# Gated MLP beside a scan: more feature tiles by block products, their operand sums in larger jobs

## The chip, the cores and the metric

The kernel runs on one core of a Trainium2 chip. Four engines compute: TensorE multiplies matrices, VectorE and ScalarE work element by element, GpSimd does the same on SBUF alone; SyncE issues the DMAs. SBUF is the on-chip memory (128 partitions), PSUM the accumulators that TensorE writes, HBM the memory behind the DMAs. The metric is device time in microseconds (us), the median of several runs.

## The reference

The input x is (8, 512, 512): eight batches of 512 rows, layer-normalised to xn. Two branches read xn, and the output is x plus their product.

```
xn = layernorm(x)
s  = ssm_branch(xn)              # input projection, conv, selective scan, output projection
g  = silu(ffn_branch(xn))
out = x + s * g

ffn_branch:  attn = causal attention(rmsnorm(xn) * ln1);  mod = 0.1 * tanh(attn @ A)
             h    = rmsnorm(xn) * ln2
             gate = silu(h @ W_in.T + mod * (h @ A) @ B)       # 2048 features
             up   = h @ W_up.T
             ffn  = xn + (gate * up) @ W_down.T
```

Products are fp32 made of three passes: each operand is a high part (fp32r, the form TensorE multiplies) and a low part, and high*high, high*low and low*high are summed in PSUM.

## The kernel before

The scan branch and the attention come first and are not touched. The gated MLP (gate, up, down) follows. Its 2048 features are 16 tiles of 128, and the eight batches have 512 rows each. A tile of one batch is called a step here.

Tiles 0 to 7 are computed directly, batch after batch (64 steps; four run inside the attention). In a step TensorE makes the gate and the up projection (`column`, helper `project3`, lines 72 to 74: 12 matmuls each, one more for the modulation at L2229), ScalarE the silu (L2279) and the high part GH (L2282), VectorE the product with up (L2302, which also frees the up bank) and the low part GL (L2304), and TensorE the 12 down matmuls (L2253 to L2255): 37 matmuls. After a batch's last step VectorE adds the sums in PSUM to the scaled skip rows (L2319) and SyncE stores them to `m_scratch`. SyncE loads the rows of each batch (FH, FL, 1 MB each) and the skip rows XT once a batch.

Tiles 8 to 15 are computed by a block scheme: two tiles and two batches form a 2x2 block matrix over halves of the 512 inputs, and seven products of blocks replace eight (the form with sums s1 to s4 of weight blocks and t1 to t4 of row blocks). One such group of 7 products for gate and for up, with modulation and 48 down matmuls, has 136 matmuls and stands for four steps of 37. There are 4 pairs of batches (`PAIRS`) times 4 pairs of tiles (`UNITS`): 16 block products. Each adds its down sums to MP in SBUF (`evict`, L2704), and after the last of a pair the rows are finished (silu, times s, plus x) and stored.

The operands of these products are sums of blocks, split in high and low. They are made during the direct steps, in `jobs`: 16 for rows (`rows`), 16 for weights (`weights`) and 4 for the down weights (`outward`), each in a buffer JOB of 8 KB a partition, two buffers in turn. SyncE loads a job (`load_job`, L2350 to L2359), GpSimd sums and splits it (`do_job`, L2385 to L2417), and SyncE stores the parts to scratch (`keep_job`, L2374, L2376), from where the block products load them as XB, SW and DW.

The order of everything is written out by hand in the generator `ffn_order`; every engine walks through the same list and does its part of each entry. SyncE therefore issues DMAs strictly in that order, and a DMA that waits for a semaphore holds all behind it. Before the first block product `second_ahead` waits until all jobs are stored, and loads XB0 to XB2 and SW0.

## Time and profile before

| | us |
|---|---|
| median of 3 runs | 2480.52 (2477.16 to 2482.77) |
| the profiled execution | 2479.31 |
| its span, first to last instruction | 2477.3 |
| TensorE busy | 2400.3 (97%) |
| VectorE, ScalarE, GpSimd busy | 1498.7, 1108.8, 708.8 |

In a row of the profile the columns are: start, duration, engine (PE is TensorE, DVE VectorE, ACT ScalarE, POOL GpSimd, SPq the queue of SyncE), line of the kernel, operation, tile written and tiles read, shape, count; in brackets the idle time before it and what ended that. Buffer numbers are left out of tile names (JOB stands for every JOB buffer). A busy PE means that matmuls follow each other without a gap: their recorded durations overlap, and the pitch from start to start is what a matmul costs.

### The profile page before, as it was taken

The page shows a single profiled execution, that of the slowest core. Times are in us where ns is not written, and L with a number is a line of the kernel's source. Part 1 is how long each engine was busy: PE and PEld are TensorE (multiplying, and loading weights), DVE is VectorE, ACT ScalarE, POOL GpSimd, SP SyncE. Part 2 cuts the span into 40 slices and gives each one's busy share as a digit, 9 for nine tenths or more (in the row PEclk, how much of TensorE's full clock was granted, in tenths as well). Part 3 has the DMA queues.
Part 4 walks back from the last instruction along what each step waited for, and adds up shares of the span by engine and source line. Part 5 has one row for each costly group of instructions (what it writes and reads, how often), then busy time and mean ns, then how long its engine had stood idle before and what let it go on. Part 6 is the DMA issues. An engine that isn't in the chain of part 4 may idle for free.

```text
span 2477.3 us, 37647 instructions
## 1 busy us (share of the span) xinstructions
PE 2400.3 (97%) x13847; PEld 1944.4 (78%) x13847; DVE 1498.7 (60%) x3000; ACT 1108.8 (45%) x1895; POOL 708.8 (29%) x674
## 2 busy tenths in 40 slices
PE   7999999999999899999999999999999999999998
PEld 5878878778888777777777678888888887787876
DVE  7857667667565588888988853223332345454546
ACT  6444544544444377777777641111111233332333
POOL 4000000000001244454453616664647002121212
PEclk9999999999999999999999899999999999999999
DMA  4000100000003577676666426655555945555461
GB/s 146 18 35 1 35 18 18 35 18 18 17 1 107 184 208 215 201 201 192 178 182 201 129 77 208 217 198 188 194 199 175 351 174 205 203 189 219 163 245 68
DMA packets 190747, 348.65 MB, mean 141 GB/s; under 512 B 19008, under 2 KB 89664, under 8 KB 181840
## 3 DMA queue, kind: packets, MB, share of 16 engines
q1 hardware_dynamic: 188064, 345.91, 42.6%
q8 instruction: 112, 1.84, 0.3%
q10 hardware_dynamic: 2496, 0.29, 0.1%
q14 instruction: 75, 0.61, 0.1%
HBM read 234.70 MB, written 111.15 MB: 140 GB/s over the span
## 4 chain that ended last, share of the span: by engine, by line
PE 80%; DVE 7%; issue 5%; DMA 4%; ACT 2%; POOL 2%; SPq 1%; DVEq 0%; ACTq 0%; POOLq 0%
PE PS L72 12%; PE PS L74 12%; PE PS L73 12%; PE PS L1748 3%; PE PS L813 2%; PE PS L812 2%; PE PS L814 2%; PE PS L2253 2%; PE PS L2254 2%; PE PS L2255 2%; PE PS L1706 2%; PE PS L1725 2%; PE PS L1707 2%; PE PS L1708 2%; PE PS L2612 2%
## 5 line engine op out<-in xcount | busy, mean ns | idle before, releaser
L1912 DVE CUSTOM_DVE_ANT_0 PS<-PS,MK 128x512 f32<-128x512 f32 (+3 forms) x512 | 244.4, 503 | 70.5 <-PE PS L1725 68.7
L1848 ACT ACTIVATE PF<-PS 128x512 f32<-128x512 f32 (+1 forms) x384 | 201.0, 528 | 90.5 <-PE PS L1752 60.0
L2302 DVE TENSOR_TENSOR SG<-SG,PS 128x512 f32<-128x512 f32 x60 | 41.3, 688 | 290.9 <-PE PS L74 289.7
L72 PE MATMUL PS<-XH,WH 128*128 128x512 f32 x504 | 208.8, 414 | 0.0
L74 PE MATMUL PS<-XH,WL 128*128 128x512 f32 x504 | 197.6, 392 | 0.0
L73 PE MATMUL PS<-XL,WH 128*128 128x512 f32 x504 | 196.8, 390 | 0.0
L74 PE MATMUL PS<-FH,GU 128*128 128x512 f32 x480 | 187.9, 391 | 0.0
L73 PE MATMUL PS<-FL,GU 128*128 128x512 f32 x480 | 187.5, 391 | 0.0
L72 PE MATMUL PS<-FH,GU 128*128 128x512 f32 x480 | 187.4, 390 | 0.0
L1725 PE MATMUL PS<-KS,QS 96*128 96x512 f32 (+3 forms) x512 | 172.4, 352 | 13.2 <-DVE MX L1912 13.1
L72 PE MATMUL PS<-XB,SW 128*128 128x512 f32 x448 | 175.5, 392 | 4.4 <-ACT P L2669 3.6
L1917 DVE TENSOR_TENSOR PL<-PF,PH 128x1024 f16<-128x1024 f32 (+1 forms) x128 | 175.4, 1370 | 4.1 <-ACT PH L1853 4.1
L74 PE MATMUL PS<-XB,SW 128*128 128x512 f32 x448 | 175.3, 391 | 0.0
L73 PE MATMUL PS<-XB,SW 128*128 128x512 f32 x448 | 175.0, 391 | 0.0
L1748 PE MATMUL PS<-QS,KS 97*128 97x512 f32 (+3 forms) x512 | 170.1, 374 | 0.0
L1089 DVE SCALAR_TENSOR_TENSOR XC<-PS,CW,XC 128x511 f32<-128x511 f32 (+2 forms) x192 | 143.6, 748 | 33.6 <-ACT XC L950 28.6
L1853 ACT CAST PH<-PF 128x1280 f16<-128x1280 f32 x128 | 161.2, 1260 | 4.1
L2012 POOL TENSOR_TENSOR PL<-PF,PH 128x256 f16<-128x256 f32 x112 | 91.8, 819 | 190.9 <-ACT PH L1853 190.6
L2279 ACT ACTIVATE SG<-PS 128x512 f32<-128x512 f32 x60 | 36.0, 601 | 243.4 <-PE PS L2229 243.3
L2764 POOL TENSOR_TENSOR U<-U,P 128x512 f32<-128x512 f32 x16 | 20.8, 1297 | 386.5 <-ACT P L2669 386.5
L657 POOL TENSOR_TENSOR RSTD<-VT,MHALF 128x4 f32<-128x4 f32 x8 | 8.1, 1012 | 417.9 <-DVE VT L576 417.9
L1725 PEld LDWEIGHTS PS<-KS,QS 96*128 96x128 f32 x512 | 100.6, 203 | 27.1 <-DVE MX L1912 22.1
(352 smaller groups left out, 6644.5 us busy)
## 6 DMA issues: line engine op xcount, KB each, us to landing
SW<-sw_scratch SPq DMA_DIRECT2D x10, 3584.0 KB, 12.3
qk_scratch<-QT SPq DMA_DIRECT2D x128, 256.0 KB, 4.7
QS<-qk_scratch SPq DMA_DIRECT2D x96, 256.0 KB, 4.0
KS<-qk_scratch SPq DMA_DIRECT2D x96, 256.0 KB, 4.0
xt_scratch<-JOB SPq DMA_DIRECT2D x32, 512.0 KB, 3.5
XB<-xt_scratch SPq DMA_DIRECT2D x16, 1024.0 KB, 6.3
sw_scratch<-JOB SPq DMA_DIRECT2D x32, 448.0 KB, 3.3
DW<-dw_scratch SPq DMA_DIRECT2D x10, 1024.0 KB, 5.0
```

The lines of the kernel that those rows point to most:

```text
L72: pe.matmul(o, lh(k), xh(k), start=open_ and k == 0, stop=False, skip_group_check=True)
L73: pe.matmul(o, lh(k), xl(k), start=False, stop=False, skip_group_check=True)
L74: last = pe.matmul(o, ll(k), xh(k), start=False, stop=close and k == nk - 1, skip_group_check=True)
L812: pe.matmul(PS[bank][:, :], YH[u][:, c], OH[:, d, :], start=d == 0, stop=False, skip_group_check=True)
L1089: dve.scalar_tensor_tensor(out=y[:, j:], in0=p[:, 0:S - j], scalar=CW[:, d, 3 - j:4 - j], in1=y[:, j:], op0=ALU.mult, op1=ALU.add).then_in ...
L1725: t = pe.matmul(PS[2 + a % 2][:, at:at + n], QS[0:96, h, 128 * how:n], KS[0:96, h, 0:n], start=how != 1, stop=True, skip_group_check=True)
L1748: t = pe.matmul(p[:, at:at + n], KS[0:97, h, 128 * J:128 * J + 128], QS[0:97, h, 128 * J:512], start=len(how) == 2 and at == 0, stop=len(h ...
L1848: act.activation(PE_[u][:, o:o + at], PS[4 + a % 2][:, 0:at], ACT.Exp, scale=SC).then_inc(a_ex, 1)
L1853: act.copy(PH[u][:, :], PE_[u][:, :]).then_inc(a_ph, 1)
L1912: dve.tensor_tensor_reduce(out=p, in0=p, in1=MK[:, 512 - n:512], scale=1.0, scalar=NEG, op0=ALU.add, op1=ALU.max, accum_out=MX[w % 2][:, j ...
L1917: dve.tensor_tensor(PL[u][:, 0:n], PE_[u][:, 0:n], PH[u][:, 0:n], ALU.subtract).then_inc(a_rm, 1)
L2012: pool.tensor_tensor(PL[u][:, 1024:1280], PE_[u][:, 1024:1280], PH[u][:, 1024:1280], ALU.subtract).then_inc(a_rp, 1)
```

## The change

Twelve tiles instead of eight are computed by block products: `FIRST` is 4 tiles directly and `UNITS` 6, so 24 block products instead of 16, and 32 direct steps (four inside the attention) instead of 64. The loads, scalings and splits of tiles 4 to 7 among the direct ones (`slice`) go. The jobs become 8 for rows, 12 for weights and 6 for down weights, in four buffers of 16 KB a partition: two for weights and down weights (class 0, `JOB0` and `JOB1`, summed by GpSimd) and two for rows (class 1, `JOB2` and `JOB3`, summed by VectorE in three parts, in three successive steps: L2377 to L2380, L2383 to L2387, L2390). A job's load is issued in the step after the store of the job that had its buffer, and still waits for that store to land. In the block product the extra modulation matmul goes to the bank DN[0] instead of ZG, and the first down matmul waits for the VectorE add that reads it.

```diff
-        GU.append(sb(re_, "GU1", [128, 4, 4, 512], F32R))
+        sb(re_, "GAP", [128, 8192])
+        js = ExitStack()
+        sb(js, "KEPT3", [128, 29576])
+        JOB = [sb(js, f"JOB{i}", [128, 4096], F32R) for i in range(2)]
+        sb(js, "KEPT4", [128, 4096])
+        JOB.append(sb(js, "JOB2", [128, 4096], F32R))
+        sb(js, "KEPT5", [128, 4096])
+        JOB.append(sb(js, "JOB3", [128, 4096], F32R))
+        js.close()
...
-        PAIRS, UNITS = NB // 2, 4
+        PAIRS, UNITS, FIRST = NB // 2, 6, 4
         ORDER = [u if p % 2 == 0 else UNITS - 1 - u for p in range(PAIRS) for u in range(UNITS)]
-        rows_jobs = [[("rows", p, k, t) for k in range(2) for t in range(2)] for p in range(PAIRS)]
-        unit_jobs = [[("weights", u, j, k) for j in range(2) for k in range(2)] + [("outward", u, 0, 0)] for u in range(UNITS)]
-        jobs = [job for u in range(UNITS) for job in rows_jobs[u] + unit_jobs[u]]
+        jobs = [[job for u in range(UNITS) for job in (("weights", u, 0), ("weights", u, 1), ("outward", u, 0))],
+                [("rows", p, k) for p in range(PAIRS) for k in range(2)]]
...
-            yield "slice", 6
+            yield "skips_scaled", 0
+            for w in range(2):
+                for n in range(2):
+                    yield "job_load", (w, n)
             yield "down", 3
-            ahead = 0
-            for q in range(EARLY + 1, 8 * NB):
-                b, f = divmod(q, 8)
+            later = {}
+            for q in range(EARLY + 1, FIRST * NB):
+                b, f = divmod(q, FIRST)
                 yield "column", q
                 yield "product", q
                 yield "down", q - 1
                 if f == 0 and b + 1 < NB:
                     yield "rows", b + 1
-                if f == 1 and b:
+                if f == 1:
                     yield "skips", b
-                if f == 6:
+                    if b == 1:
+                        yield "rows", 2
+                if f == 3:
                     yield "skips_scaled", b
-                if q == EARLY + 1:
-                    yield "slice", 7
-                if q >= 8 and q % 3 and ahead < len(jobs):
-                    if ahead == 0:
-                        yield "job", 0
-                    if ahead + 1 < len(jobs):
-                        yield "job", ahead + 1
-                    yield "job_kept", ahead
-                    ahead += 1
-            assert ahead == len(jobs)
+                i = q - EARLY - 1
+                for w, n in later.pop(i, ()):
+                    yield "job_load", (w, n)
+                if i % 4 == 0 and i // 4 < UNITS:
+                    for n in range(3 * (i // 4), 3 * (i // 4) + 3):
+                        yield "job", (0, n)
+                if i // 3 < len(jobs[1]):
+                    yield "job", (1, (i // 3, i % 3))
+                kept = []
+                if i >= 2 and i % 4 != 1 and (i - 2) // 4 < UNITS:
+                    kept.append((0, 3 * ((i - 2) // 4) + (i - 2) % 4))
+                if i and i % 3 == 0 and i // 3 <= len(jobs[1]):
+                    kept.append((1, i // 3 - 1))
+                for w, n in kept:
+                    yield "job_kept", (w, n)
+                    if n + 2 < len(jobs[w]):
+                        later.setdefault(i + 1, []).append((w, n + 2))
             yield "second_half", 0
-            yield "down", 8 * NB - 1
+            yield "down", FIRST * NB - 1
...
+        def load_job(sp, w, n):
+            kind, a, j = jobs[w][n]
+            r = 2 * w + n % 2
+            J = f32(JOB[r][:, :])
             if n >= 2:
-                sp.wait_ge(j_st[n % 2], j_st0[n % 2] + 32 * (n // 2))
-            else:
+                sp.wait_ge(j_st[r], j_st0[r] + 32 * (n // 2))
+            elif n == 0:
...
+                        c = 2048 * x + 1024 * b
+                        sp.dma_start(J[:, c:c + 1024].rearrange("p (k t) -> p k t", k=2),
+                                     f32(rows[2 * a + b])[:, j::2, :]).then_inc(j_ld[r], 16)
...
+                    sp.dma_start(J[:, 512 * f:512 * f + 512], (WgT, WuT)[j][FIRST + 2 * a + f]).then_inc(j_ld[r], 16)
...
+                    sp.dma_start(J[:, 512 * f:512 * f + 512], wd_[FIRST + 2 * a + f]).then_inc(j_ld[r], 16)
...
+                high, low = (J[:, c:c + 2048].rearrange("p (i t) -> p i t", i=4) for c in (0, 2048))
+                to = [f32(xt_d[a])[:, :, x, j, :] for x in range(2)]
...
+                high, low = (J[:, c:c + 1792] for c in (2048, 0))
+                to = [f32(sw_d[a])[:, j, x, :, :, :].rearrange("p i k m -> p (i k m)") for x in range(2)]
...
+                high, low = (J[:, c:c + 1024].rearrange("p (f m) -> p f m", f=2) for c in (2048, 0))
                 to = [f32(dw_d[a])[:, :, x, :] for x in range(2)]
...
+            sp.wait_ge(j_op[w], j_op0[w] + job_ops(w, n) - 1)
+            sp.dma_start(to[0], high).then_inc(j_st[r], 16)
+            sp.wait_ge(j_op[w], j_op0[w] + job_ops(w, n))
+            sp.dma_start(to[1], low).then_inc(j_st[r], 16)
...
+        def sum_rows(dve, n, part):
+            r, op, op0 = 2 + n % 2, j_op[1], j_op0[1] + 7 * n
+            R_, J = JOB[r][:, :], f32(JOB[r][:, :])
+            b11, b21, b12, b22, t1, t2, t3, t4 = (J[:, 512 * i:512 * i + 512] for i in range(8))
+            if part == 0:
+                dve.wait_ge(j_ld[r], j_ld0[r] + job_loads(1, n))
+                dve.tensor_tensor(J[:, 0:2048], J[:, 0:2048], J[:, 2048:4096], ALU.add).then_inc(op, 1)
+                dve.wait_ge(op, op0 + 1)
+                dve.tensor_tensor(t1, b12, b11, ALU.subtract).then_inc(op, 1)
+                dve.tensor_tensor(t3, b22, b12, ALU.subtract).then_inc(op, 1)
+            elif part == 1:
+                dve.wait_ge(op, op0 + 2)
+                dve.tensor_tensor(t2, b22, t1, ALU.subtract).then_inc(op, 1)
+                dve.wait_ge(op, op0 + 4)
+                dve.tensor_tensor(t4, b21, t2, ALU.subtract).then_inc(op, 1)
+                dve.wait_ge(op, op0 + 5)
+                dve.tensor_copy(R_[:, 0:2048], J[:, 2048:4096]).then_inc(op, 1)
             else:
...
+                dve.wait_ge(op, op0 + 6)
+                dve.tensor_tensor(R_[:, 2048:4096], J[:, 2048:4096], J[:, 0:2048], ALU.subtract).then_inc(op, 1)
...
+        def sum_weights(pool, n):
+            kind, a, j = jobs[0][n]
+            r, op, op0 = n % 2, j_op[0], j_op0[0] + (job_ops(0, n - 1) if n else 0)
+            R_, J = JOB[r][:, :], f32(JOB[r][:, :])
+            pool.wait_ge(j_ld[r], j_ld0[r] + job_loads(0, n))
+            if kind == "weights":
+                w0, w1 = (J[:, c:c + 512].rearrange("p (k m) -> p k m", k=4) for c in (0, 512))
+                a11, a12, a21, a22, s1, s2, s4 = (J[:, 256 * i:256 * i + 256] for i in range(7))
+                pool.tensor_tensor(w0, w0, l2b(), ALU.mult).then_inc(op, 1)
+                pool.tensor_tensor(w1, w1, l2b(), ALU.mult).then_inc(op, 1)
+                pool.wait_ge(op, op0 + 2)
+                pool.tensor_tensor(s1, a21, a22, ALU.add).then_inc(op, 1)
+                pool.wait_ge(op, op0 + 3)
+                pool.tensor_tensor(s2, s1, a11, ALU.subtract).then_inc(op, 1)
+                pool.wait_ge(op, op0 + 4)
+                pool.tensor_tensor(s4, a12, s2, ALU.subtract).then_inc(op, 1)
+                pool.tensor_tensor(a21, a11, a21, ALU.subtract).then_inc(op, 1)
+                pool.wait_ge(op, op0 + 6)
+                pool.tensor_copy(R_[:, 2048:3840], J[:, 0:1792]).then_inc(op, 1)
+                pool.wait_ge(op, op0 + 7)
+                pool.tensor_tensor(R_[:, 0:1792], J[:, 0:1792], J[:, 2048:3840], ALU.subtract).then_inc(op, 1)
+            else:
+                pool.tensor_copy(R_[:, 2048:3072], J[:, 0:1024]).then_inc(op, 1)
+                pool.wait_ge(op, op0 + 1)
+                pool.tensor_tensor(R_[:, 0:1024], J[:, 0:1024], J[:, 2048:3072], ALU.subtract).then_inc(op, 1)
...
+            for r in range(4):
+                sp.wait_ge(j_st[r], j_st0[r] + 32 * len(range(r % 2, len(jobs[r // 2]), 2)))
+            sp.wait_ge(m_u, FIRST * NB - FIRST)
...
-                pe.wait_ge(n_ad, n_ad0 + 5 * v + 1)
-                modulate(pe, ZG, f1, b1, True).then_inc(n_pr, 1)
+                pe.wait_ge(*((n_ev, 8 * v - 3) if v else (m_fn, 4 * NB - 1)))
+                modulate(pe, DN[0], f1, b1, True).then_inc(n_pr, 1)
...
-                    if t < 2:
-                        pe.wait_ge(*((n_ev, 8 * v - 3 + t) if v else (m_fn, 4 * NB - 1 + t)))
+                    if t == 0:
+                        pe.wait_ge(n_ad, n_ad0 + 5 * v + 3)
...
```

On SyncE, in the second batch of direct steps in which jobs run, the order before is this. `a_q` and `a_k` are semaphores of landed stores, `a_lg` counts GpSimd's operations, `m_fn` VectorE's additions at the end of a batch.

```order
L2350 DMA JOB0<-rh_scratch 128x2x256 [waits a_q]
L2350 DMA JOB0<-rh_scratch 128x2x256
L2350 DMA JOB0<-rl_scratch 128x2x256 x2
L2374 DMA xt_scratch<-JOB1 512x1x256 [waits a_lg]
L2376 DMA xt_scratch<-JOB1 512x1x256 [waits a_lg]
L2350 DMA JOB1<-rh_scratch 128x2x256 [waits a_k]
```

The same place now, from the store of the first rows job on; `a_nu` counts VectorE's operations on row jobs, and `a_wt` is a semaphore of landed stores too.

```order
L2367 DMA xt_scratch<-JOB2 512x1x512 [waits a_nu]
L2369 DMA xt_scratch<-JOB2 512x1x512 [waits a_nu]
L2201 DMA XT0<-in_x_dram 128x512 [waits m_fn]
L2201 DMA XT1<-in_x_dram 128x512 [waits m_fn]
L2201 DMA XT2<-in_x_dram 128x512 [waits m_fn]
L2201 DMA XT3<-in_x_dram 128x512 [waits m_fn]
L2348 DMA JOB1<-in_WgT_dram 128x512 [waits a_k]
L2348 DMA JOB1<-in_WgT_dram 128x512
L2344 DMA JOB2<-rh_scratch 128x2x512 [waits a_wt]
L2344 DMA JOB2<-rh_scratch 128x2x512
L2344 DMA JOB2<-rl_scratch 128x2x512 x2
L2367 DMA dw_scratch<-JOB0 256x1x512 [waits a_lg]
```

Both classes of jobs now share the one queue, transfers are twice as long a row, and a load of rows stands behind loads and stores of weights.

On VectorE, around the end of a batch, the direct steps before:

```order
L2302 TENSOR_TENSOR SG0<-SG0,PS2 128x512 [waits m_u,m_sg]
L2304 TENSOR_TENSOR GL0<-SG0,GH0 128x512 [waits m_gh]
L2319 TENSOR_TENSOR M10<-XT0,PS4 128x512 [waits m_m0,m_xn,a_th,m_dn]
L2319 TENSOR_TENSOR M11<-XT1,PS5 128x512 [waits m_xn,m_m1]
L2319 TENSOR_TENSOR M12<-XT2,PS6 128x512 [waits m_xn,m_m2]
L2319 TENSOR_TENSOR M13<-XT3,PS7 128x512 [waits m_xn,m_m3]
L2302 TENSOR_TENSOR SG1<-SG1,PS3 128x512 [waits m_u,m_sg]
```

And now, from the last of these additions on; `a_ni` and `a_ti` are semaphores of landed loads of row jobs.

```order
L2311 TENSOR_TENSOR M13<-XT3,PS7 128x512 [waits m_xn,m_m3]
L2377 TENSOR_TENSOR JOB3<-JOB3 128x2048 [waits a_ni]
L2379 TENSOR_TENSOR JOB3<-JOB3 128x512 [waits a_nu]
L2380 TENSOR_TENSOR JOB3<-JOB3 128x512
L2292 TENSOR_TENSOR SG1<-SG1,PS3 128x512 [waits m_u,m_sg]
L2294 TENSOR_TENSOR GL1<-SG1,GH1 128x512 [waits m_gh]
L2383 TENSOR_TENSOR JOB3<-JOB3 128x512 [waits a_nu]
L2385 TENSOR_TENSOR JOB3<-JOB3 128x512 [waits a_nu]
L2387 CAST JOB3<-JOB3 128x2048 [waits a_nu]
```

Seven operations of a row job, the first of which waits for a DMA, now stand in VectorE's queue between the products of the steps.

## Rows read from the trace of the kernel before

**Rows 1.** Busy time by stage: stretch, length, busy us of each engine, PEclk, DMA share, GB/s

```profile
1458.00:1958.00 500.00, 500.00 (x2193) 412.03 (x2193) 159.73 (x190) 76.42 (x126) 261.60 (x248) 1.00 0.58 195
1958.00:2477.00 519.00, 499.64 (x2179) 408.44 (x2178) 263.34 (x373) 170.39 (x288) 90.39 (x63) 0.99 0.52 193
```

**Rows 2.** Waits in 1458 to 2477: engine, line, releaser: total us, times, longest

```profile
DVE SG L2302 <- PE PS L74: 289.7, 57, 6.4
...
PE PS L2612 <- DVE HH L2743: 4.5, 3, 1.5
PE PS L72 <- ACT P L2669: 3.6, 3, 1.2
```

**Rows 3.** TensorE in order of time: first direct step that remains, first block product

```profile
1457.84 0.39 PE L72 MATMUL PS<-FH,GU 128*128 128x512 f32 x1
...
1958.52 0.39 PE L72 MATMUL PS<-XB,SW 128*128 128x512 f32 x1
...
2009.66 0.39 PE L2612 MATMUL PS<-DW,HH 128*128 128x512 f32 x1
```

**Rows 4.** VectorE in order of time: end of modulation, two steps, two block products

```profile
1456.55 0.68 DVE L1958 TENSOR_TENSOR MS<-PS,MS 16x512 fp32r<-16x512 f32 x1 [3.05 <-ACT MS L1882]
...
1522.91 0.69 DVE L2302 TENSOR_TENSOR SG<-SG,PS 128x512 f32<-128x512 f32 x1 [6.37 <-PE PS L74]
...
1531.35 0.69 DVE L2302 TENSOR_TENSOR SG<-SG,PS 128x512 f32<-128x512 f32 x1 [5.40 <-PE PS L74]
...
2000.96 0.69 DVE L2712 TENSOR_TENSOR G<-G,PS 128x512 f32<-128x512 f32 x1 [10.54 <-PE PS L74]
...
2007.69 0.67 DVE L2728 TENSOR_TENSOR U<-U,PS 128x512 f32<-128x512 f32 x1
...
2031.97 0.69 DVE L2712 TENSOR_TENSOR G<-G,PS 128x512 f32<-128x512 f32 x1 [10.54 <-PE PS L74]
```

**Rows 5.** DMA in 4 us from 2224.4, then from 1632.4, then from 2140.4

```profile
DMA packets 835, 1.53 MB, mean 382 GB/s; under 512 B 90, under 2 KB 90, under 8 KB 835
q1 hardware_dynamic: 835, 1.53, 103.0%
...
DMA packets 215, 1.63 MB, mean 408 GB/s; under 512 B 16, under 2 KB 16, under 8 KB 16
...
DMA packets 64, 1.84 MB, mean 459 GB/s; under 512 B 0, under 2 KB 0, under 8 KB 0
```

**Rows 6.** SyncE's queue: the second store of a job, the load behind it

```profile
1525.42 0.55 SPq L2376 DMA_DIRECT2D xt_scratch<-JOB  x1
1528.85 1.22 SPq L2350 DMA_DIRECT2D JOB<-rh_scratch  x2
```

**Rows 7.** GpSimd in order of time, operations of the jobs

```profile
1648.25 0.73 POOL L2390 TENSOR_TENSOR JOB<-JOB 128x256 f32<-128x256 f32 x1
...
1653.78 0.62 POOL L2401 TENSOR_TENSOR JOB<-JOB,L2C 128x256 f32<-128x256 f32 x1
...
1657.07 0.93 POOL L2411 CAST JOB<-JOB 128x896 fp32r<-128x896 f32 x1
1658.09 2.12 POOL L2413 TENSOR_TENSOR JOB<-JOB 128x896 fp32r<-128x896 f32 x1
```

**Rows 8.** GpSimd and VectorE in order of time, one operation of each

```profile
1709.67 2.40 POOL L2417 TENSOR_TENSOR JOB<-JOB 128x1024 fp32r<-128x1024 f32 x1
...
1709.96 2.66 DVE L2304 TENSOR_TENSOR GL<-SG,GH 128x512 fp32r<-128x512 f32 x1 [0.69 <-ACT GH L2282]
```

**Rows 9.** DMA issues on the page: engine, count, KB each, us to landing

```profile
SW<-sw_scratch SPq DMA_DIRECT2D x10, 3584.0 KB, 12.3
...
DW<-dw_scratch SPq DMA_DIRECT2D x10, 1024.0 KB, 5.0
```

**Rows 10.** Three stretches of TensorE: length, busy us, PEclk, DMA share, GB/s

```profile
1390.00:1394.00 4.00, 3.50 (x41) 1.00 0.69 238
1394.00:1398.00 4.00, 0.66 (x4) 0.74 0.01 2
1398.00:1402.00 4.00, 4.00 (x22) 0.50 0.42 136
```

More of the change, by code:

```diff
@@ L2192, in ffn_sync @@
                         sp.dma_start(XT[u][:, :], xn_[4 * n + u]).then_inc(m_t[u], 16)
-                elif kind == "job":
-                    load_job(sp, n)
+                elif kind == "job_load":
+                    load_job(sp, *n)
                 elif kind == "job_kept":
-                    keep_job(sp, n)
+                    keep_job(sp, *n)
                 elif kind == "second_half":
                     second_ahead(sp)
-                elif kind == "down" and n % 8 == 7:
-                    h = n // 8
+                elif kind == "down" and n % FIRST == FIRST - 1:
+                    h = n // FIRST
                     for u in range(4):
@@ L2310, in ffn_vector @@
                                           ALU.subtract, ALU.mult).then_inc(m_xn, 1)
-                elif kind == "down" and q % 8 == 7:
-                    h = q // 8
+                elif kind == "job" and q[0] == 1:
+                    sum_rows(dve, *q[1])
+                elif kind == "down" and q % FIRST == FIRST - 1:
+                    h = q // FIRST
                     dve.wait_ge(m_dn, q + 1)
@@ L2325, in ffn_pool, with job_loads, job_ops @@
                     attn_pool(pool, [("inverse", n, None)])
-                elif kind == "job":
-                    do_job(pool, n)
+                elif kind == "job" and n[0] == 0:
+                    sum_weights(pool, n[1])
             second_pool(pool)
-        def job_loads(n):
-            return sum(64 if jobs[i][0] == "rows" else 32 for i in range(n % 2, n + 1, 2))
-        def job_ops(n):
-            return sum({"rows": 7, "weights": 8, "outward": 2}[jobs[i][0]] for i in range(n + 1))
-        def load_job(sp, n):
-            kind, a, j, k = jobs[n]
-            J = f32(JOB[n % 2][:, :])
+        def job_loads(w, n):
+            return (32, 64)[w] * (n // 2 + 1)
+        def job_ops(w, n):
+            return sum({"rows": 7, "weights": 8, "outward": 2}[jobs[w][i][0]] for i in range(n + 1))
+        def load_job(sp, w, n):
+            kind, a, j = jobs[w][n]
+            r = 2 * w + n % 2
+            J = f32(JOB[r][:, :])
             if n >= 2:
-                sp.wait_ge(j_st[n % 2], j_st0[n % 2] + 32 * (n // 2))
-            else:
+                sp.wait_ge(j_st[r], j_st0[r] + 32 * (n // 2))
+            elif n == 0:
                 sp.wait_ge(a_mo, 2 * NB)
@@ L2361, in keep_job @@
[L2361 to L2363 removed]
+                    sp.dma_start(J[:, 512 * f:512 * f + 512], wd_[FIRST + 2 * a + f]).then_inc(j_ld[r], 16)
+        def keep_job(sp, w, n):
+            kind, a, j = jobs[w][n]
+            r = 2 * w + n % 2
+            J = f32(JOB[r][:, :])
             if kind == "rows":
[L2365 to L2366 removed]
+                high, low = (J[:, c:c + 2048].rearrange("p (i t) -> p i t", i=4) for c in (0, 2048))
+                to = [f32(xt_d[a])[:, :, x, j, :] for x in range(2)]
@@ L2431, in load_unit @@
         def load_unit(sp, u, free):
-            if free is None:
-                sp.wait_ge(m_u, 60 if u == 0 else 8 * NB)
-            else:
+            if free is None and u:
+                sp.wait_ge(m_u, FIRST * NB)
+            elif free is not None:
                 sp.wait_ge(n_pr, 15 * (free + 1))
@@ L2437, in load_unit @@
                          f32(sw_d[u]).rearrange("p a b c d e -> p (a b c d e)")).then_inc(n_sw[u % 2], 16)
-            if free is None:
-                sp.wait_ge(m_dn, 58 + 2 * u)
-            else:
+            if free is not None:
                 sp.wait_ge(n_dd, 8 * (free + 1))
@@ L2480, in second_ahead @@
         def second_ahead(sp):
-            for r in range(2):
-                sp.wait_ge(j_st[r], j_st0[r] + 32 * len(range(r, len(jobs), 2)))
-            sp.wait_ge(m_u, 56)
+            for r in range(4):
+                sp.wait_ge(j_st[r], j_st0[r] + 32 * len(range(r % 2, len(jobs[r // 2]), 2)))
+            sp.wait_ge(m_u, FIRST * NB - FIRST)
             for i in range(3):
@@ L2760, in second_pool @@
                 if v and v % UNITS == 0:
-                    for n in range(2 * v - 8, 2 * v):
+                    for n in range(8 * (v // UNITS) - 8, 8 * (v // UNITS)):
                         skipped(n)
```

173 lines of the change are left out of this document (46 added, 127 removed).

## The prediction

> **What bounds the kernel now.** I read the busy time by stage first. From 1458 to 1958 us (direct steps) TensorE is busy all 500.00 us at the full granted clock, from 1958 to 2477 (block products) 499.64 of 519; VectorE has 160 and 263 us of work there, GpSimd 262 and 90, and the DMA engines are busy 0.58 and 0.52 of the time [rows 1]. The list of waits says the same from the other side: VectorE waits 289.7 us for TensorE, while TensorE's two waits for others are 4.5 and 3.6 us in all, at the three ends of a pair [rows 2]. So the matmuls' pitch is the bound, and DMAs and sums hide behind it. The reader should keep the two middle figures in mind: 195 GB/s now [rows 1], and no packet size of this kernel that goes far beyond 400 GB/s [rows 5].
>
> The profiled execution took 2479.31 us, its span of 2477.3 and 2.0 around it; the median is 1.2 above it, which is inside the scatter of the runs. I count from the span.
>
> **TensorE.** VectorE's product of one step and that of the next are 1531.35 - 1522.91 = 8.44 us apart, those of two block products 2031.97 - 2000.96 = 31.01 [rows 4]. Each of the 8 new block products takes the place of four steps: 31.01 - 4 x 8.44 = -2.75 us, by eight -22.0. (136 matmuls for 148, 12 x 0.228 = 2.74, agrees.) The first remaining direct step starts at 1457.84 [rows 3]; 27 of the 32 steps follow from there. 27 steps of 8.44 and some 2.7 for the last step's down matmuls (12 x 0.228) bring the first block product to 1688.4 if nothing holds TensorE, and the end of the span to 2455.3.
>
> **Slices and DN[0].** The scalings and splits of tiles 4 to 7 that go ran on engines that wait for TensorE: 0. The wait for DN[0] costs nothing by the old place: the VectorE add that it waits for ends at 2008.36 [rows 4], 1.3 us before the first down matmul at 2009.66 [rows 3]; plus or minus 1 us at the four pair ends. With six products to a pair, one SW and one DW load, 12.3 and 5.0 us [rows 9], lie in 31.0 us: hidden, 0.
>
> **DMA in the direct stage.** Here the change does most. The direct stage shrinks from 500 us to 231, but its bytes don't. The first job loads stand behind the end of the modulation (1456.55 + 0.68 [rows 4]), so everything below falls between 1457.2 and the first block product, which needs SW0, and SW0 stands behind the last store of the jobs:
> - in packets of 2 KB: eight row jobs, 2.10 MB in and 2.10 out, 33.6 MB; weight loads 12 x 0.52 = 6.3; down weights 6 x 1.57 = 9.4; seven batches of skip rows, 7.3; seven stores of M1, 7.3. Together 64.0 MB;
> - in larger packets: weight stores 12 x 1.835 = 22.0 MB, rows of batches 2 to 7 12.6, XB0 to XB2 3.1, SW0 3.7. Together 41.4.
>
> 105.3 MB in 231 us would be 456 GB/s, with no idle moment. With the queue full this trace shows 382 GB/s for 2 KB packets, 408 for the larger ones of the steps, and 459 only for the 28 KB packets of SW [rows 5]. So: 64.0/0.385 = 166 us (I take 385, as the short view's 382 has its edges in it), 22.0/0.408 = 54, 12.6/0.408 = 31, 3.1/0.400 = 8, 3.7/0.455 = 8: 267 us.
>
> To it come stretches in which the queue is empty. SyncE waits for a store to land before it may issue the load that takes the buffer, and holds all behind it: after the second store of a job was issued the next load came 3.43 us later [rows 6], of which the transfer is 1.4, so 2.0 us idle. Of 22 such gates I find seven where the store awaited was the last thing issued (behind weight jobs 2, 5, 11 and 14, row jobs 2 and 3, and before the first XB): 14 us. At the start SyncE stands at the M1 stores of a batch until TensorE has finished it: 6 us. Landing of SW0: 1.5. 267 + 14 + 6 + 1.5 = 288.5, so the first block product starts at 1745.7 instead of 1688.4: +57.
>
> TensorE can't run ahead of this: sums of row jobs stand in VectorE's queue between the products that free the PSUM banks, so a row load that is late by more than some 8 us stops the steps; and what is not held there is held before the first block product. Bounds: everything at 459 GB/s and no gate gives 1457.2 + 229.4 + 7.5 = 1694, +6; everything at 2 KB rates with the wait of 2.0 at all 22 gates 1457.2 + 276 + 44 + 7.5 = 1785, +96.
>
> A rule of the notes bears on this rate. The Trainium skill, "DMA: Bandwidth & Descriptors", section Bandwidth, has large transfers measured at 341 GB/s for 1 MB and 425 for 16 MB. By 425 the 105.3 MB take 248 us and the kernel ends near 2485, by 341 they take 309 and it ends near 2546, each without the terms that follow; the trace's 382 to 408 lies between them.
>
> **GpSimd late with a sum.** A weight job is two scalings of 512 (1.24 each), four sums of 256 (0.73), a cast of 1792 (1.86) and a subtraction of 1792 (4.24), twice the widths of [rows 7] where they doubled: 10.3, with gaps 11.4 us. Down weights 3.5; a unit 26.3. When an operation of VectorE on SBUF overlaps, one of the two stands still: GL took 2.66 us beside a GpSimd subtraction [rows 8], and 0.69 is usual. Now VectorE sums rows there too: 16 widths of 512 at 0.67 [rows 4] are up to 10.7 us a job. With these between, I take 16.5 us for a weight job. SyncE then comes to its store before it is summed in four places of every twelve steps, by some 3, 4.5, 4.5 and 8 us: 20 us for a repetition. Twelve steps are half of the job schedule, which would make 40; part of it is taken up by gates and start already counted. I take +20, bounds 0 and +40.
>
> **Restart.** The first block products come after TensorE has stood still, and DMAs of the first pair (XB3 behind DW0 and the eight MP loads) are late by some 2.5 us. After a stretch with 0.66 us of work in 4 the granted clock was 0.74 and then 0.50, that is 1.2 of 2.4 GHz [rows 10]. I take +4, bounds 0 and +8.
>
> **Sum.** 2477.3 - 22.0 + 57 + 20 + 4 = 2536.3; with 2.0 outside 2538 us. The far ends of all terms are 2463 and 2601. The forecast's own range is 2500 to 2575.
>
> **Rivals.**
> - *The DMAs keep pace.* TensorE stays gapless and only the -22.0 counts: 2457 us, up to 2475 if the first pair starts late. For it: DMA is at 0.58 now, and no store in the old stage holds TensorE. Against: it needs 456 GB/s through the whole stage, and 61% of the bytes are in packets that were never seen above 385. Chance 0.07.
> - *DMA bound, but gates and sums hide.* If all packets go at 408 or a little better and deeper backlog covers the gates, the stage takes 105.3/0.408 + 7.5 = 265.6 us, the first block product starts at 1722.8, +34: 2491, and 2476 at the better end, where gain and loss are about even. For it: four buffers and loads issued a step late leave more in the queue than before. Against: six of the seven gates follow directly from the order. Chance 0.11, 0.04 of it for no change.
> - *The engines' exclusion is the bound.* GpSimd's 26.3 us, 4/3 row jobs of VectorE (14.3) and its four GL (2.8) are 43.4 us for four steps of 33.8, if they never overlap; with some 8 us more in which sums wait for transfers and not the other way round, 51. Six units: 6 x (51 - 33.8) = 103, in place of 57 + 20: 2455.3 + 2.0 + 103 + 6 + 4 = 2570, to 2600 with the gates. For it: [rows 8]. Against: that row is one pair of operations, and most of VectorE's operations there read PSUM. Chance 0.14. The Trainium skill, "SBUF — State Buffer", calls the shared ports an exclusive lock whose loser fully blocks; [rows 8] agrees for this one pair.
>
> **How the numbers follow.** The forecast has 0.68. A measurement here tells 0.2% (5 us) from no change. Faster: 0.07, the first rival; same: 0.04, the better end of the second; slower: all else, 0.89. The range from 2480 to 2592 leaves out the first rival, the second's best end, and the far end of the third.
>
> **What would show it.** Right: the stage from 1458 to the first block product lasts some 288 us, with DMA busy 0.9 or more at about 370 to 385 GB/s; TensorE has gaps in it that end with VectorE's product, which stood behind a row sum that waited for its load; SyncE's longest waits are for landed stores and for GpSimd's sums; block products keep 31.0 us. The lock is the bound instead if DMA share stays near 0.75 while GpSimd's subtractions last 6 us and more and VectorE's casts several us. Wrong altogether: a direct stage of about 231 us with TensorE gapless, or block products that last longer than 31 us.

## The result, and the profile after

The changed kernel takes 2538.52 us (2537.01 to 2540.75), the kernel before on the same chip 2479.15 (four runs; 2480.52 above was the median of three): a ratio of 1.0239, 95% interval 1.0221 to 1.0256. The prediction was 2538. The profiled execution has a span of 2536.1 us.

The busy time by stage of the kernel after [rows 1 has it for before]: the direct steps until the first block product, the last part of that stretch by itself, and the block products.

```profile
1738.00:1767.50 29.50, 0.00 (x0) 0.00 (x0) 4.57 (x8) 0.00 (x0) 0.00 (x0) 0.54 0.95 374
1457.00:1767.50 310.50, 238.60 (x999) 192.37 (x998) 190.85 (x174) 32.08 (x54) 173.32 (x108) 0.90 0.91 340
1767.50:2536.10 768.60, 748.87 (x3264) 613.82 (x3264) 378.05 (x537) 246.57 (x416) 113.22 (x79) 0.99 0.49 185
```

TensorE, gapless in that stage before, has 71.9 us of gaps there now, 29.5 of them at the end, where it does nothing at all. The DMA engines are busy 0.91 of the stage, at 340 GB/s where it was 195. The block products are as they were: 768.6 us for 24 against 518.8 for 16 [rows 3 and the span], 31.2 for each of the eight new ones. VectorE's rows there answer to [rows 4], at the same pitch of 31.01; the add of U3 (L2727) ends at 2009.31, 1.3 us before the first down matmul (L2611 now) at 2010.63, as before.

```profile
2001.92 0.69 DVE L2711 TENSOR_TENSOR G<-G,PS 128x512 f32<-128x512 f32 x1 [10.54 <-PE PS L74]
2008.64 0.67 DVE L2727 TENSOR_TENSOR U<-U,PS 128x512 f32<-128x512 f32 x1
2032.93 0.69 DVE L2711 TENSOR_TENSOR G<-G,PS 128x512 f32<-128x512 f32 x1 [10.54 <-PE PS L74]
```

```profile
2010.63 0.39 PE L2611 MATMUL PS<-DW,HH 128*128 128x512 f32 x1
```

The waits of the kernel after from 1455 to 1800 us, in total, times and longest [rows 2 has before's]. L2259 is the first down matmul of a step, L2294 VectorE's GL, L2311 the additions of M1, L2377 the first sum of a row job.

```profile
DVE JOB L2377 <- DMA JOB<-rl_scratch: 48.0, 7, 12.5
...
PE PS L72 <- DMA SW<-sw_scratch: 31.3, 1, 31.3
PE PS L2259 <- DVE GL L2294: 23.8, 5, 14.6
...
PE PS L2259 <- DVE M L2311: 15.4, 3, 7.6
```

VectorE stands at row sums for their loads, TensorE for VectorE, and at the end TensorE for SW0. SyncE's own waits in that stretch: L2212 are the M1 stores, L2344 to L2351 loads that wait for a store to land, L2369 a store that waits for a sum.

```profile
SPq L2348 <- DMA sw_scratch<-JOB: 30.4, 4, 10.1
SPq L2212 <- DVE M L2311: 30.3, 12, 20.8
SPq L2348 <- DMA dw_scratch<-JOB: 28.3, 5, 8.8
SPq L2344 <- DMA xt_scratch<-JOB: 18.9, 4, 8.5
SPq L2369 <- POOL JOB L2412: 17.0, 6, 5.7
```

The DMA queue of the kernel after from 1457 to 1767.5: packets, MB, share of the 16 engines.

```profile
q1 hardware_dynamic: 39295, 105.31, 91.0%
```

105.31 MB, as predicted, in 0.910 x 310.5 = 282.6 us of transfer, 373 GB/s where I had counted 267 us. (The Trainium skill, "DMA: Bandwidth & Descriptors", section Bandwidth, has 341 and 425 GB/s measured for loads of 1 and 16 MB; the 373 lies between.)

### The profile page after: what moved, and what is told of

It is laid out like the page before. It is cut to its first block, busy times and chain, and to the rows that moved or that the text cites. A ratio compares the mean times of both kernels' runs of the same rounds, so it can differ in the third digit from the quotient of the medians.

```text
span 2536.1 us, 37627 instructions
## 1 busy us (share of the span) xinstructions
PE 2387.7 (94%) x13751; PEld 1929.0 (76%) x13751; DVE 1639.1 (65%) x3140; ACT 1137.7 (45%) x1947; POOL 643.6 (25%) x550
## 4 chain that ended last, share of the span: by engine, by line
PE 69%; DMA 9%; DVE 8%; issue 5%; POOL 3%; SPq 3%; ACT 2%; DVEq 0%; ACTq 0%; POOLq 0%
PE PS L72 10%; PE PS L74 10%; PE PS L73 10%; PE PS L2611 3%; PE PS L2612 3%; PE PS L2613 3%; PE PS L1748 2%; PE PS L813 2%; PE PS L812 2%; PE PS L814 2%; PE PS L1706 2%; DMA xt_scratch<-JOB 2%; PE PS L1725 2%; PE PS L1707 2%; PE PS L1708 2%
## 5 line engine op out<-in xcount | busy, mean ns | idle before, releaser
L72 PE MATMUL PS<-XB,SW 128*128 128x512 f32 x672 | 264.0, 393 | 34.9 <-DMA SW<-sw_scratch 31.3
L74 PE MATMUL PS<-XB,SW 128*128 128x512 f32 x672 | 263.4, 392 | 0.0
L73 PE MATMUL PS<-XB,SW 128*128 128x512 f32 x672 | 263.1, 392 | 0.0
L2763 POOL TENSOR_TENSOR U<-U,P 128x512 f32<-128x512 f32 x24 | 31.9, 1329 | 607.2 <-ACT P L2668 607.2
L2711 DVE TENSOR_TENSOR G<-G,PS 128x512 f32<-128x512 f32 x24 | 16.5, 687 | 249.5 <-PE PS L74 249.5
L72 PEld LDWEIGHTS PS<-XB,SW 128*128 128x128 f32 x672 | 126.7, 189 | 65.5 <-DMA SW<-sw_scratch 31.7
L2703 DVE TENSOR_TENSOR MP<-MP,PS 128x512 f32<-128x512 f32 x192 | 129.2, 684 | 72.2 <-PE PS L2613 72.1
L2611 PE MATMUL PS<-DW,HH 128*128 128x512 f32 x384 | 149.6, 390 | 5.3 <-DVE U L2727 5.3
L2613 PE MATMUL PS<-DW,HH 128*128 128x512 f32 x384 | 149.4, 389 | 0.0
L2612 PE MATMUL PS<-DW,HH 128*128 128x512 f32 x384 | 149.4, 389 | 0.0
L73 PEld LDWEIGHTS PS<-XB,SW 128*128 128x128 f32 x672 | 126.8, 189 | 27.5
L74 PEld LDWEIGHTS PS<-XB,SW 128*128 128x128 f32 x672 | 126.9, 189 | 27.2
## 6 DMA issues: line engine op xcount, KB each, us to landing
sw_scratch<-JOB SPq DMA_DIRECT2D x24, 896.0 KB, 10.3
```

What stands on the lines that cost most here:

```text
L72: pe.matmul(o, lh(k), xh(k), start=open_ and k == 0, stop=False, skip_group_check=True)
L73: pe.matmul(o, lh(k), xl(k), start=False, stop=False, skip_group_check=True)
L74: last = pe.matmul(o, ll(k), xh(k), start=False, stop=close and k == nk - 1, skip_group_check=True)
L2611: pe.matmul(bank[:, :], high, DW2[u % 2][:, f, 0, :], start=f == 0, stop=False, skip_group_check=True)
L2612: pe.matmul(bank[:, :], high, DW2[u % 2][:, f, 1, :], start=False, stop=False, skip_group_check=True)
L2613: last = pe.matmul(bank[:, :], low, DW2[u % 2][:, f, 0, :], start=False, stop=f == 1, skip_group_check=True)
```

## The experiments

Theory D: the stage is bound by its 105 MB of transfers. Theory L: by GpSimd and VectorE shutting each other out. Theory Q: by SyncE's order, in which loads wait for landings, stores for sums, and M1 stores for TensorE. Theory R, formed after the first four runs, is one loop of Q. D+Q, formed after e8, has transfers and order side by side, each covering what the other gives back. The runs come from four sessions, each beside the kernel before on the same chip (medians 2476.1 to 2479.4), so they are compared by their ratios. "First block product" is its place in the profiled execution; MB and share are those of the DMA queue from 1457 us to there, as in the row above.

| | ratio to before | first block product | MB, share |
|---|---|---|---|
| the changed kernel | 1.0239 (1.0221 to 1.0256) | 1767.5 | 105.3, 0.91 |
| e1 sums 32 wide | 1.0249 (1.0231 to 1.0267) | 1757.2 | 104.6, 0.93 |
| e2 fewer bytes | 1.0137 (1.0112 to 1.0162) | 1734.1 | 76.4, 0.76 |
| e3 rows from SBUF | 1.0255 (1.0236 to 1.0275) | 1762.2 | 88.1, 0.78 |
| e4 8 KB stores | 1.0252 (1.0235 to 1.0269) | 1765.6 | 105.3, 0.90 |
| e5 third buffer | 1.0262 (1.0239 to 1.0284) | 1768.8 | 105.8, 0.91 |
| e7 = e3 + e5 | 1.0202 (1.0178 to 1.0226) | 1753.6 | 88.9, 0.81 |
| e8 = e7 + late M1 stores | 1.0109 (1.0085 to 1.0132) | 1730.1 | 88.1, 0.85 |
| e9 late M1 stores only | 1.0216 (1.0193 to 1.0240) | 1762.1 | 105.9, 0.91 |
| e10 = e8 + first loads early | 1.0126 (1.0103 to 1.0148) | 1721.1 | 82.7, 0.84 |
| e13 = e8 + fewer bytes | 1.0075 (1.0057 to 1.0092) | 1733.6 | 65.9, 0.65 |
| e11 six tiles direct | 0.9993 (0.9982 to 1.0004) | | |
| e12 = e11, sums spread | 1.0001 (0.9992 to 1.0010) | 1829.9 | |

**e1_sums_32_wide.** All sums of jobs narrow, here the longest two of VectorE:

```diff
-                dve.tensor_tensor(J[:, 0:2048], J[:, 0:2048], J[:, 2048:4096], ALU.add).then_inc(op, 1)
+                dve.tensor_tensor(J[:, 0:32], J[:, 0:32], J[:, 2048:2080], ALU.add).then_inc(op, 1)
...
-                dve.tensor_copy(R_[:, 0:2048], J[:, 2048:4096]).then_inc(op, 1)
+                dve.tensor_copy(R_[:, 0:32], J[:, 2048:2080]).then_inc(op, 1)
```

> All sums of jobs keep their number and order but are 32 columns wide (GpSimd's first two jobs whole), so they take almost no time; every load and store is as in the changed kernel. The scratch operands are not the reference's. Theory D (the direct stage is bound by its 105 MB of DMA; the engines' exclusion costs only the stretches in which SyncE waits for a sum): of the 34 us in which the DMA engines lack work some 8 to 20 go, 2518 to 2530 us. Theory L (GpSimd and VectorE shut each other out, and that sets the stage): the whole loss of some 77 us goes, 2478 or less.

Measured 2534.96, ratio 1.0249: no change. GpSimd's work in the stage fell from 173 to 44 us, VectorE's from 191 to 87, and the time stayed, above D's 2518 to 2530 too. While 105 MB go, the sums are not the bound: L falls for the changed kernel, and with it my term of +20 for late sums as an addition. What the sums cost once the bytes are fewer e1 can't say. The stage by engine and the DMA queue of e1 from 1457 to 1757.2:

```profile
1457.00:1757.20 300.20, 238.40 (x988) 191.93 (x986) 87.09 (x171) 31.74 (x53) 43.81 (x106) 0.91 0.93 349
```

```profile
q1 hardware_dynamic: 38929, 104.59, 93.1%
```

0.931 x 300.2 = 279.5 us of transfer: with the sums gone the transfers fill what was left. (The profiled execution was the shortest of e1's four, 2527.24, so the first block product at 1757.2 flatters it.)

**e2_a_third_fewer_bytes.**

```diff
-                high, low = (J[:, c:c + 1792] for c in (2048, 0))
+                m = 448 if a else 1792
+                high, low = (J[:, c:c + m] for c in (2048, 0))
```

> All sums whole, all DMAs in their number, order and waits, but from the second unit and pair on the stores carry a quarter (down weights whole), row loads half of their bytes: about 75 MB instead of 105 until the first block product. The block products read the first unit's and the first pair's operands, in size as before. Theory D: 75 MB at 360 to 380 GB/s are 197 to 208 us, under the 231 that TensorE needs, so most of the loss goes: 2459 to 2480 us. Theory L: sums are as wide as before, 2525 or more. Theory Q (SyncE's order: a load waits for a store to land, a store for a sum, whatever the bytes): each of 22 gates keeps its 2 us and the waits for sums stay, some 2500 to 2515.

2508.54, ratio 1.0137: some 25 us of 60 come back, less than D had said and inside what Q had. Against the changed kernel it is the only run that takes away nothing but bytes, 29 MB of 105.

**e3_rows_from_sbuf.**

```diff
-                dve.tensor_tensor(J[:, 0:2048], J[:, 0:2048], J[:, 2048:4096], ALU.add).then_inc(op, 1)
+                for x in range(2):
+                    dve.wait_ge(m_r[x], 32 * (a + 1) - (0 if x else 16))
+                    dve.tensor_tensor(J[:, 1024 * x:1024 * x + 1024].rearrange("p (k t) -> p k t", k=2),
+                                      f32(FH[x])[:, j::2, :], f32(FL[x])[:, j::2, :], ALU.add).then_inc(op, 1)
```

> Row jobs add FH and FL of both batches of a pair where they lie in SBUF, instead of loading the same rows again: 16.8 MB of loads and eight gates less, sums as wide as before, outputs the reference's. Theory D: 16.8 MB at 359 GB/s are 47 us, and 88.5 MB take some 234, about what TensorE needs; with 10 to 20 us of gates and start 2466 to 2490 us. Theory L: the same VectorE and GpSimd work on SBUF, 2530 or more. Theory Q: the eight gates of the row loads and what stands behind them, 15 to 25 us, so 2513 to 2523.

2535.99, ratio 1.0255: nothing, although 17 MB less went. D alone falls too; Q's 2513 to 2523 is missed as well, and only L's "2530 or more" holds, which e1 speaks against. But the edit does more than take loads away: the two row jobs of a pair are now summed within five steps of every eight, and since the sums read FH and FL, SyncE may load a later batch's rows only after them, which is a new wait. SyncE's waits in e3 until 1762.2 (L2221 M1 stores, L2357 weight loads, L2377 and L2379 job stores, L2204 the rows of batch 2, which here wait for VectorE's sum):

```profile
SPq L2221 <- DVE M L2320: 36.2, 12, 20.2
SPq L2357 <- DMA sw_scratch<-JOB: 31.7, 5, 10.8
SPq L2379 <- POOL JOB L2432: 30.9, 8, 4.6
SPq L2377 <- POOL JOB L2430: 30.4, 7, 6.1
SPq L2357 <- DMA dw_scratch<-JOB: 29.7, 5, 9.3
SPq L2204 <- DVE JOB L2396: 12.5, 1, 12.5
```

They add up to 171 us of a stage of 305, while the DMA engines are busy only 0.78 of it. The loads that went are missing where SyncE stands longest: from 1460 to 1500 the DMA share is 0.44 in e3 and 0.82 in the changed kernel, with the new wait of 12.5 us and one of 20.2 at the M1 stores in that stretch. How much of the 17 MB's gain the new wait took was not tried. And the weight jobs run in a loop. e3 in order of time, the last store of a unit's second weight job, the load that waits for it to land, and GpSimd's first sum on that load:

```profile
1593.33 0.56 SPq L2379 DMA_DIRECT2D sw_scratch<-JOB  x1
...
1606.61 0.80 SPq L2357 DMA_DIRECT2D JOB<-in_WgT_dram  x2
...
1610.55 1.23 POOL L2420 TENSOR_TENSOR JOB<-JOB,L2C 128x512 f32<-128x512 f32 x1 [3.92 <-DMA JOB<-in_WgT_dram]
```

Three jobs a unit in two buffers: the next unit's first weight job gets the buffer of the one summed last, 17 us from store to sum. The DMA queue was busy 0.965 of the 22 us from 1590 on, so most of these 17 us are transfers of other loads and stores.

**e4_xt_8_kb_stores.**

```diff
-        xt_d = nc.dram_tensor("xt_scratch", [4, 128, 4, 2, 2, S], F32R, kind="Internal").ap()
+        xt_d = nc.dram_tensor("xt_scratch", [4, 128, 2, 2, 4, S], F32R, kind="Internal").ap()
```

> The scratch of the row jobs is laid out so that a store writes 8 KB a partition in one piece instead of four of 2 KB; the loads of XB1 to XB6 read 2 KB pieces instead. Bytes, sums and waits stay. Theory D with packets as the price: 16.8 MB of stores at 400 to 408 instead of 359 GB/s are 4 to 6 us less in the direct stage, XB1 and XB2 give back 0.7: 2533 to 2535 us, and the block products stay at 31.0. Theories L and Q: 2538, within 1.5.

2537.27, ratio 1.0252. A gain of 4 us would not stand out from this scatter, so the time is inconclusive on the price of packets. The queue's own row shows it: 33923 packets instead of 39295, and 0.901 x 308.5 = 278.0 us of transfer instead of 282.6, about what was expected. It is the time that did not follow.

**e5_third_buffer.** (third buffer in the place of STGC; load and store counts follow)

```diff
-            r = 2 * w + n % 2
+            r = 2 + n % 2 if w else (0, 1, 4)[n % 3]
```

> The changed kernel with a third buffer for class 0 (12 KB a partition in the place of STGC, which is dead by then): a unit's two weight jobs and its down weights each have a buffer, so the load of the next unit's first weight job no longer waits for the store of the second one. Bytes, sums and operations stay. Theory R (ring: the two buffers and three jobs a unit make a loop of load, two sums, landing of the store, load, of some 42 us in e3 and 46 to 48 in the changed kernel, against 33.8 of four steps; the transfers of 105 MB, some 281 us, are a second bound of about the same size): the ring goes, the transfers stay, first block product 1745 to 1757, 2513 to 2527 us. Theory D alone (bytes): 2530 to 2540, as e3 should have fallen by then and didn't, so it is weak. Theory Q (SyncE's waits for sums and landings in general): 2530 or more.

2543.00, ratio 1.0262: a miss for R, nothing gained; Q had 2530 or more. With all bytes on the way the loop isn't what is late.

**e7_rows_from_sbuf_third_buffer.** Both edits.

> e3 (rows from SBUF, 16.8 MB less) and e5 (third buffer) together, outputs the reference's. Theory R with the second bound: both are relieved, 88.5 MB in some 236 us, with 15 to 30 us of start and gates the first block product at 1708 to 1723: 2477 to 2492 us, that is 45 to 60 less than either part alone leaves. Theory Q: SyncE's standing at M1 stores and at sums stays, 2505 to 2525.

2527.60, ratio 1.0202. Neither edit alone gained; together they give some 9 us (1.0239 to 1.0202 of 2479, with intervals that just overlap), far from the 45 to 60 expected of R, and 3 us above Q's range too. The loop is a small part of Q.

**e8_both_late_m1_stores.**

```diff
+                if f == 0:
+                    yield "skips_kept", b - 1
...
-                elif kind == "down" and n % FIRST == FIRST - 1:
-                    h = n // FIRST
+                elif kind == "skips_kept":
+                    h = n
```

> e7 with the M1 stores of a batch at the end of SyncE's part of that step instead of in front of its loads and job stores (SyncE stood there for 20 us in the first batch and 30 to 36 in all). Theory R: the first down weights load and the first stores go out some 15 us earlier, 5 to 12 us less than e7, 2468 to 2485. Theory Q: 20 us and more less than e7.

2504.59, ratio 1.0109: 23 us less than e7, by nothing but the place of a batch's four small stores in one queue, as Q had said. SyncE's wait at them fell from 69.4 us in e7 to 11.3; a part of it moved to the wait that e3's edit brought in, for VectorE's row sums ahead of a batch's rows, 12.4 us in e7:

```profile
SPq L2212 <- DVE JOB L2404: 28.2, 3, 12.8
SPq L2229 <- DVE M L2328: 11.3, 11, 4.9
```

**e9_only_late_m1_stores.** The same edit on the changed kernel.

> The changed kernel with only the M1 stores moved to the end of SyncE's part of a step (the edit that gave 23 us from e7 to e8). Theory D+Q (two paths of about the same length side by side: the transfers, 281 us when all 105 MB go, and SyncE's order with its standing at M1 stores, sums and landings; each alone covers what the other gives back): only the start goes, where the DMA engines idled 6.5 us, so 2528 to 2537 us. Theory Q alone (SyncE's order sets the stage): 20 us and more, 2518 or less.

2531.22, ratio 1.0216: 5.7 us by the ratios, with intervals that overlap. The edit worth 23 us in e8 is worth a quarter of that by the medians while 105 MB go: here transfers cover the order. This is inside the 2528 to 2537 that D+Q had said beforehand, and above Q's 2518.

**e10_first_loads_early.**

```diff
+                if i == 25:
+                    yield "first_loads", 0
```

> e8, and SW0 and XB0 to XB2 are loaded as soon as the weight jobs that shared their place are stored, ahead of the last row stores, DW0 and MP; the load of batch 2's rows stands behind the first job's store (SyncE waited there 12.8 us for VectorE). Theory D+Q: TensorE's wait of 22 us before the first block product in e8 shrinks to some 5, and the start gains a few us: 2482 to 2492 us. If transfers are still the bound at the end of the stage, the wait only moves into the first pair (XB3, DW0, MP): 2495 to 2505.

2508.32, ratio 1.0126, not better than e8, and above both ranges expected. TensorE of e10, from 1700 to 1800:

```profile
1721.06 0.76 PE L72 MATMUL PS<-XB,SW 128*128 128x512 f32 x1 [6.07 <-issue]
1749.08 0.79 PE L72 MATMUL PS<-XB,SW 128*128 128x512 f32 x1 [16.87 <-DMA XB<-xt_scratch]
```

The first block product comes 9 us earlier than in e8, and TensorE waits 16.87 us for the next XB instead: the wait moved into the first pair, the way of the second case, 3 us past its range.

**e13_e8_third_fewer_bytes.** e2's cut of the stores on e8.

> e8 (twelve tiles, row sums from SBUF, third buffer, late M1 stores) with the cut of e2's stores: from the second unit and pair on a quarter of their bytes, some 65 MB instead of 88. The block products read the first unit's and pair's operands. Theory D+Q (transfers and SyncE's order together were the whole loss): TensorE's 231 us are the bound, first block product at 1690 to 1702, 2459 to 2471 us, which shows TensorE's term of -22. If the sums or their exclusion hold TensorE, 2480 or more.

2499.69, ratio 1.0075: a miss for D+Q; "2480 or more" was the case in which sums hold TensorE. (The profiled execution was the longest of e13's four, and e8's the shortest of its four.) The queue and TensorE's waits until 1733.5:

```profile
q1 hardware_dynamic: 26317, 65.91, 65.2%
```

```profile
PE PS L2276 <- DVE M L2328: 13.3, 3, 6.4
PE PS L2276 <- DVE GL L2311: 9.8, 1, 9.8
```

22 MB less than e8 bring some 8 us, with intervals that overlap and the DMA engines idle a third of the time. What holds TensorE there is VectorE, 23.1 us of waits, whose products stand behind row sums, and SW0. SyncE's longest wait in e13 is for the row sums too, the one that e3's edit brought in:

```profile
SPq L2212 <- DVE JOB L2406: 47.8, 3, 19.8
```

In the longest of the three, from 1597.5 to 1617.4, the DMA engines are busy 0.09 of the time, VectorE 19.1 us of 19.9 and GpSimd 17.2, and VectorE's four scalings of XT take 8.15 us where one takes 0.56 on average in e1. So theory L, which e1 excludes for the changed kernel, stands again as a rival for what is left here. Of the changed kernel's 59 us some 40 are shown to belong to bytes and SyncE's order; which edit would bring the rest is open. e1's narrow sums were not tried on e13, and no run cut bytes to 66 MB without the new wait.

**e11_six_tiles_direct.** Ten tiles by block products.

```diff
-        PAIRS, UNITS, FIRST = NB // 2, 6, 4
+        PAIRS, UNITS, FIRST = NB // 2, 5, 6
```

> Ten tiles by block products instead of twelve: six direct tiles (48 steps), five units, 20 block products, row sums from SBUF as in e3, M1 stores late as in e8, one buffer for weight jobs, one for down weights, one for rows; outputs the reference's. By TensorE's term alone 4 x -2.75 = -11.0 against the kernel before: 2466 of span, 2468 us, if the stage of 43 steps (363 us for some 85 MB, 235 GB/s) hides all transfers and sums; TensorE then has no gap over 2 us. Theory D+Q: nothing is late with that much room, 2466 to 2474. If VectorE's row sums hold TensorE at the ends of batches even so, 2475 to 2485.

2475.41 against 2476.77 of the kernel before, ratio 0.9993: the same, where 11 us less were expected.

**e12_six_tiles_sums_spread.**

```diff
-                for x in range(3):
-                    row_parts[12 * p - 3 + 4 * n + x] = [(2 * p + n, x)]
+                row_parts[12 * p - 2 + 4 * n] = [(2 * p + n, 0)]
+                row_parts[12 * p - 1 + 4 * n] = [(2 * p + n, 1), (2 * p + n, 2)]
```

> e11 (six direct tiles, ten by block products) with the row sums of the first pair a step apart from each other's stores (the second row job starts at step 3, its parts follow at 6 and 7, batch 2's rows are loaded at step 3) and those of the later pairs in steps in which GpSimd has no weight job, down weights a step earlier, row stores first in SyncE's part of a step. In e11 three stalls of TensorE (2.05, 2.72, 2.17 us) and the halved clock behind them took 11 us between 1500 and 1600 us, as much as the four block products give. Without them 2464 to 2470 us; if VectorE and GpSimd still meet, 2471 to 2476.

2479.42, ratio 1.0001: a miss. TensorE of e12, and the stretch of 100 us around its first wait, then the same stretch of the kernel before:

```profile
1566.54 0.79 PE L2293 MATMUL PS<-DW,GH 128*128 128x512 f32 x1 [3.24 <-DVE GL L2342]
...
1772.68 0.50 PE L2293 MATMUL PS<-DW,GH 128*128 128x512 f32 x1 [1.39 <-DVE GL L2342]
...
1841.59 0.50 PE L72 MATMUL PS<-XB,SW 128*128 128x512 f32 x1 [3.20 <-DMA XB<-xt_scratch]
```

```profile
1500.00:1600.00 100.00, 96.76 (x419) 79.26 (x418) 60.24 (x57) 13.93 (x23) 43.52 (x27) 0.98 0.55 200
```

```profile
1500.00:1600.00 100.00, 100.00 (x440) 82.38 (x440) 27.58 (x31) 14.44 (x24) 68.41 (x64) 1.00 0.67 219
```

440 matmuls before, 419 in e12. One wait of 3.24 us cost 21 x 0.228 = 4.8 us: its next matmul is recorded with 0.79 us instead of 0.39. The same count, matmuls missing against the pitch of 0.228, gives 0.5 us from 1600 to 1700, 1.6 to 1800, 0.7 to 1829.9 and 5.2 to 1860, where the wait for XB is: with the first some 13 us, against the 12 by which the span of 2478.5 misses the 2466 that TensorE's term gives. The pair ends cost what they did before (9.2 us of waits, 8.9 before). So in this execution the waits and the clock behind them account for about all of the loss. Neither version beats the kernel before.

## Why the prediction was right, point by point

The forecast of 2538 met the time. Its main mechanism held, that the bytes of the jobs no longer fit into the shorter stage (e2); that late sums and gates add to the transfers did not (e1, e8, e9), and that the total came out all the same is luck.

**TensorE, -22.0.** Held: 31.2 us for each new block product where 31.01 was counted, and the same pitch. But no run shows the -22 alone, since no kernel with twelve tiles has a median under 2499.

**DN[0] and the slices, 0.** Held. The waits at the pair ends are 5.3 and 2.5 us where before they were 4.5 and 3.6 [rows 2]:

```profile
PE PS L2611 <- DVE U L2727: 5.3, 3, 1.8
PE PS L72 <- ACT P L2668: 2.5, 3, 1.0
```

**Transfers, +57.** The bytes were right (105.31 for 105.3 MB), the speed was not: 373 GB/s over the stage instead of 394 (105.3 in 267 us), so 282.6 us. The share of 0.91 came as named, the 370 to 385 GB/s only for the time in which the queue was busy; over the whole stage it was 340. A part of the error is a reading: the 382 GB/s stand beside a queue at 103.0% [rows 5], that is 371 for a full queue, and 385 was taken. (The 2485 and 2546 given beside this sum hold 7.5 us of start and landing and the +4, and leave out the 14 us of gates.)

**GpSimd late, +20.** This step failed. The lateness came: SyncE waited 25 us in all for GpSimd's sums (17.0, 6.4 and three short ones). But e1 takes it away and the time stays, so what I added to the transfers lies beside them. In the stage the queue was without work for 310.5 - 282.6 = 27.9 us, where 41.5 were counted (21.5 for gates and start, 20 here), and the transfers took 15.6 more than counted. The first block product at 1767.5 against my 1765.7 is luck: two errors of opposite sign, some 16 and some 14 us. The sum behind the 20 is wrong too: the operations of a weight job listed there add up to 11.5 us, not 10.3, and the 16.5 taken with overlaps were 13.1 on average, from first to last operation, in the trace of the kernel after.

**Gates and start, +21.5, as an addition.** Also mis-stated. I took SyncE's standing for holes in a stream of transfers. e8 and e9 show that it is a chain beside them: the same edit of the order gives 23 us where 17 MB are gone and a third buffer is in, and 6, with intervals that overlap, where all bytes go. So I read the stage as following the longer of two chains, 283 us of transfers with their few holes, and SyncE's order. For the order no run gives a length: e3's stage of 305 us at a share of 0.78 holds a wait of 12.5 us that e3 itself brings in, and in e2, with every wait of the changed kernel, the stage lasts 277. SyncE's longest wait was not for a landing or a sum, as I had said, but for the M1 stores, 20.8 us. The chains are not independent (a landing is a transfer, so fewer bytes in the stores shorten the order too), and their exact shares stay open. Of the three runs with twelve tiles whose time was expected by this reading, e9 came out as said, e10 and e13 did not; in e13 the sums may be a third chain, which no run tested. The 6 us of the start and the 1.5 of SW0's landing have no row behind them, and no run tried them alone. The +57 was no price per byte: in e2 the transfers are 72 us shorter (0.761 x 277.1 = 210.9), and 25 us come back.

**Restart, +4.** 768.6 against 766.9 us counted from the first block product: +1.7.

**The rivals.** The DMAs did not keep pace. The one by which gates hide (2491) is excluded by the time. The exclusion of VectorE and GpSimd is real for single operations (below) but by e1 not the bound of the changed kernel; with fewer bytes and the order mended it is not excluded (e13).

## What to carry to other kernels

Before work is moved from a long stage into a short one, divide the stage's bytes by its new length: 105 MB in 231 us were 456 GB/s, and the queue gave 373. Where a queue in order carries loads, stores and waits of several engines, its order is a chain by itself; count it as a rival of the transfers, not as an addition. An edit of the order brought at most 6 us while the queue was full (e5, e9) and 23 when bytes were gone (e8); fewer bytes alone brought 25 us for 29 MB (e2). An edit that removes bytes can bring in a wait of its own (e3). A right total does not show right terms: it took e1, and e8 beside e9, to tell that two of mine were wrong.
